# A fused retention layer on one core: masked scores over 512 tokens, against two chunks joined by a state, with the keys transposed by VectorE and moved by DMA

## What is computed

```python
qkv = silu(xn @ qkv_w.T)                       # q, k, v per head, 128 wide
scores = (q @ k.T) * decay                     # decay: exp(-slope_h * (n - m)) for n >= m, else 0
attn = scores @ v                              # the reference does it in blocks of 32 with a state
attn = norm_w * attn * rsqrt(mean(attn**2) + 1e-5)
x = x + (sigmoid(xn @ gate_w.T) * attn) @ out_w.T + ffn(xn)
```

## Time and profile before

| | |
|---|---|
| runs | 1080.37, 1080.43, 1080.39 us; median 1080.39 |
| profiled execution, span from the first to the last instruction | 1078.5 us (a time of its own is not listed beside it) |
| PE busy | 1072.7 us, 99% |
| weight loads of PE (beside it) | 946.2 us, 88% |
| DVE, ACT, POOL busy | 681.0, 702.6, 633.4 us (63%, 65%, 59%) |
| DMA | 60.05 MB, mean 56 GB/s |
| granted clock of PE | 1.000 |

### The profile page before, as it was taken

How to read it: one execution, slowest core, us unless ns; L and a number is a source line. 1 busy time by engine, 2 the same in 40 slices (tenths; PEclk the granted TensorE clock), 3 DMA queues, 4 the chain that set the end, 5 groups by cost and what they waited for, 6 DMA issues and landing times.

```text
span 1078.5 us, 19035 instructions
## 1 busy us (share of the span) xinstructions
PE 1072.7 (99%) x5938; PEld 946.2 (88%) x5938; DVE 681.0 (63%) x1150; ACT 702.6 (65%) x1463; POOL 633.4 (59%) x625
## 2 busy tenths in 40 slices
PE   8999999999999999999999999999999999999999
PEld 7998889888898888988898888988889888898898
DVE  6876664657556575665755666465755657566566
ACT  9677665766657665675756766576666756567642
POOL 5548563684737647375544846367473764647655
PEclk9999999999999999999999999999999999999999
DMA  8112020120202111021201102011020211102122
GB/s 304 65 45 84 25 64 21 45 64 26 64 19 70 57 34 54 7 80 39 61 26 44 63 24 63 19 44 63 24 69 14 82 44 44 45 30 77 55 90 79
DMA packets 41606, 60.05 MB, mean 56 GB/s; under 512 B 3936, under 2 KB 21600, under 8 KB 41568
## 3 DMA queue, kind: packets, MB, share of 16 engines
q1 hardware_dynamic: 41280, 59.05, 16.9%
q10 hardware_dynamic: 288, 0.52, 0.1%
HBM read 52.74 MB, written 6.82 MB: 55 GB/s over the span
## 4 chain that ended last, share of the span: by engine, by line
PE 98%; DVE 1%; ACT 0%; POOL 0%; DMA 0%; issue 0%; DVEq 0%; POOLq 0%
PE bank_q L1834 8%; PE bank_q L1836 8%; PE bank_q L1835 8%; PE bank_p L1834 6%; PE bank_p L1836 6%; PE bank_r L1834 6%; PE bank_p L1835 6%; PE bank_r L1836 6%; PE bank_r L1835 6%; PE outp L1834 5%; PE outp L1835 5%; PE outp L1836 5%; PE score L1836 3%; PE score L1835 3%; PE score L1834 3%; PE att L1836 3%
## 5 line engine op out<-in xcount | busy, mean ns | idle before, releaser
L419 POOL TENSOR_TENSOR w_lo<-combo,w_hi 128x768 fp32r<-128x768 f32 (+1 forms) x128 | 166.7, 1310 | 147.6 <-ACT w_hi L615 147.4
L419 POOL TENSOR_TENSOR w_lo<-raw,w_hi 128x256 fp32r<-128x256 f32 (+1 forms) x128 | 131.5, 1029 | 131.1 <-ACT w_hi L615 130.6
L1398 DVE TENSOR_TENSOR acc<-acc,outp 128x512 f32<-128x512 f32 x116 | 79.4, 685 | 74.7 <-PE outp L1836 73.7
L470 POOL TENSOR_TENSOR sum_sq<-sum_sq,square 128x512 f32<-128x512 f32 x64 | 82.8, 1293 | 66.6 <-ACT square L771 66.6
L1835 PE MATMUL bank_q<-c_lo,w_hi 128*128 128x512 f32 x276 | 107.4, 389 | 0.0
L1836 PE MATMUL bank_q<-c_hi,w_lo 128*128 128x512 f32 x276 | 107.4, 389 | 0.0
L1834 PE MATMUL bank_q<-c_hi,w_hi 128*128 128x512 f32 x276 | 107.4, 389 | 0.0
L615 ACT ACTIVATE p_hi<-score 128x896 fp32r<-128x896 f32 (+1 forms) x128 | 81.1, 649 | 33.9 <-DVE score L1306 33.0
L1306 DVE TENSOR_TENSOR score<-score,table 128x512 f32<-128x512 f32 (+1 forms) x128 | 75.9, 627 | 41.7 <-PE score L1836 40.7
L1257 DVE TENSOR_TENSOR xs<-bank_r,xs 128x512 f32<-128x512 f32 x64 | 44.2, 690 | 88.6 <-ACT xs L615 60.9
L1834 PE MATMUL outp<-wo_hi,g_hi 128*128 128x512 f32 x250 | 97.6, 390 | 0.0
(11 more groups left out here) (304 smaller groups left out, 3460.8 us busy)
## 6 DMA issues: line engine op xcount, KB each, us to landing
raw<-w_chunks SPq DMA_DIRECT2D x165, 256.0 KB, 2.9
near_dram<-near SPq DMA_DIRECT2D x2, 2048.0 KB, 9.8
table<-near_dram SPq DMA_DIRECT2D x32, 128.0 KB, 2.0
y<-x SPq DMA_DIRECT2D x8, 256.0 KB, 3.2
out<-acc SPq DMA_DIRECT2D x7, 256.0 KB, 2.0
acc<-x SPq DMA_DIRECT2D x6, 256.0 KB, 5.4
acc<-x ACTq DMA_DIRECT2D x2, 256.0 KB, 3.8
hw_dram<-acc SPq DMA_DIRECT2D x1, 512.0 KB, 2.6
```

Of the source, the lines that this page charges most:

```text
L419: pool.tensor_tensor(piece(w_lo[i % 2], j), piece_source(i, j), piece(w_hi[i % 2], j).bitcast(F32), ALU.subtract).then_inc(wlo[j], 1)
L470: pool.tensor_tensor(sum_sq[:, s % 2, :], sum_sq[:, s % 2, :], square[:], ALU.add).then_inc(summed, 1)
L1398: dve.tensor_tensor(tile, tile, outp, ALU.add).then_inc(acc_done, 1)
```

## The change

The 512 tokens of a sequence are cut into two chunks of 256. Within a chunk, scores and attention are done as before, in blocks of 128: per chunk one even key block against 256 queries in fp32r, and one odd block of 128x128 in plain fp32. What chunk 1 gets from chunk 0 goes through a state of 128x128:

- `turn_keys(s)` (DVE) transposes chunk 0's keys in blocks of 32x32; `move_keys(g, s)` (SP) writes them to DRAM in four DMAs, waits for these, and reads them back in two, as keys_t[token, dim];
- `keys(s)` (ACT) scales keys_t by the decay to the chunk's end; `state(s)` (PE) is keys_t times the values, in plain fp32, in the bank `side`;
- `state_high(s)` (ACT), `state_low(s)` (DVE) split it; `inter(s)` (PE) multiplies it with the queries of chunk 1;
- `fade_cross(s)` (DVE) scales that by the decay since the chunk's start (`fade`, one row per head, `load_fade` on SP), `add_cross(s)` (DVE) adds it to the second half of `att`; squares wait for att_whole.

Both chunks use one table of 256 columns, so the masks are two instructions over both, `probs` and `probs_lo` one each, and `make_far` goes. keys_t, state_hi, state_lo, cross and side exist once. All scalars and narrow tiles are moved, so that each operand of a matmul starts at a multiple of 512 bytes. The core of the diff:

```diff
+            def load_fade(head):
+                at_least(sp, cross_made, 2 * head)
+                sp.dma_start(fade[:], near_dram[bass.ds(head, 1), 0:1].rearrange("a p n -> (a p) n").to_broadcast([P, HALF])).then_inc(fade_in, 16)
+
+            def move_keys(g, s):
+                sp.wait_ge(k_turned, STEPS * g + s + 1)
+                for i in range(D // 32):
+                    sp.dma_start(keys_dram[s % 2, :, i, :].rearrange("(j t) n -> t j n", j=4),
+                                 k_blocks[32 * i:32 * i + 32, :].rearrange("t (j n) -> t j n", j=4)).then_inc(keys_out, 16)
+                sp.wait_ge(keys_out, 64 * (STEPS * g + s + 1))
+                at_least(sp, state_made, STEPS * g + s)
+                for a in range(2):
+                    sp.dma_start(keys_t[:, a, :].rearrange("p (i c) -> p i c", c=32), keys_dram[s % 2, :, :, 32 * a:32 * a + 32]).then_inc(keys_in, 16)
...
             def body(g, first=False, final=False):
+                move_keys(g, 0)
                 unit_taken(g, V1)
                 load_rows(0, 20 * g + 5, 20 * g + 6)
                 unit_taken(g, V2)
                 load_rows(1, 20 * g + 10, 20 * g + 12)
+                move_keys(g, 1)
                 load_near(4 * g + 1)
                 unit_taken(g, QK1)
                 load_rows(0, 20 * g + 8, 20 * g + 9)
+                load_fade(4 * g + 1)
                 unit_taken(g, QK2)
                 load_rows(1, 20 * g + 13, 20 * g + 17)
+                move_keys(g, 2)
+                move_keys(g, 3)
...
+                def keys(s):
+                    N, h = STEPS * g + s, s // 2
+                    act.wait_ge(keys_in, 32 * (N + 1))
+                    act.wait_ge(fades_now, g + 1)
+                    copy(keys_t[:, 0, :], keys_t[:, 0, :], scale=k_fade_now[:, 0, h:h + 1])
+                    copy(keys_t[:, 1, :], keys_t[:, 1, :], scale=k_fade_now[:, 1, h:h + 1]).then_inc(k_faded, 1)
...
+                def turn_keys(s):
...
+                    at_least(dve, keys_out, 64 * N)
+                    dve.transpose(k_blocks[:, :].rearrange("p (j a c) -> p j a c", a=2, c=32),
+                                  k_all[b][:, 0:HALF].rearrange("p (a j c) -> p j a c", a=2, c=32)).then_inc(k_turned, 1)
...
+                    at_least(pe, plo_done, N)
+                    for a in range(2):
+                        pe.matmul(score[:, a, HALF:HALF + P], k_all[b][:, a * HALF + P:a * HALF + HALF], q_odd[b][:, a, :],
+                                  start=True, stop=False, skip_group_check=True)
+                    if with_state:
+                        state(s)
+                    for a in range(2):
+                        mm = three(score[:, a, 0:HALF], k_hi[b][:, a, :], k_lo[b][:, a, :], q_hi[b][:, a * HALF:a * HALF + HALF],
+                                   q_lo[b][:, a * HALF:a * HALF + HALF], False, True)
+                    mm.then_inc(scored, 1)
...
+                def state(s):
+                    N, b, r = STEPS * g + s, s % 2, s // 4
+                    pe.wait_ge(k_faded, N + 1)
+                    at_least(pe, cross_made, N)
...
+                    for t in range(2):
+                        mm = pe.matmul(side[:, HALF:HALF + D], keys_t[:, t, :], v_01[r, b][:, t, head_cols(s)], start=t == 0, stop=t == 1,
+                                       skip_group_check=True)
+                    mm.then_inc(state_made, 1)
+
+                def inter(s):
+                    N, b = STEPS * g + s, s % 2
+                    pe.wait_ge(slo_done, N + 1)
+                    three(side[:, 0:HALF], state_hi[:], state_lo[:], q_hi[b][:, HALF:], q_lo[b][:, HALF:], True, True).then_inc(cross_ready, 1)
...
                     prod(QK2, 6)
                     output(-1)
-                    prod(QK2, 2, 5, 7)
+                    state(2)
+                    prod(QK2, 2, 5)
+                    prod(QK2, 7)
+                    inter(2)
                     attend(2)
                     prod(QK2, 4)
                     scores(3)
                     prod(QK2, 3)
                     prod(G23, 1)
+                    state(3)
```

More of the change, by code:

```diff
@@ L47 @@
 BANK_AT = {(0, 0): "p", (0, 1): "r", (1, 0): "q", (1, 1): "x"}
-P_LEN = tuple(SEQ - P * j for j in range(TB))
-P_AT = tuple(sum(P_LEN[:j]) for j in range(TB))
-P_COLS = P_AT[TB - 1]
-S_ORDER = (0, 1, 3, 2)
-A_ORDER = (0, 1, 3, 2)
-K_COLS = (TB - 1) * P
+HALF = 2 * P
 G_AT = (0, 1, 2, 0, 2, 1, 0, 2)
@@ L130, in build @@
         square = sb("square", [P, SEQ])
-        table = sb("table", [P, SEQ])
-        ident = sb("ident", [P, P])
-        ones = sb("ones", [P, 1])
-        slope = sb("slope", [P, HEADS])
-        far = sb("far", [P, 2, HEADS])
-        norm = sb("norm", [P, HEADS])
-        half_norm = sb("half_norm", [P, HEADS])
-        norm_now = sb("norm_now", [P, 4])
-        far_now = sb("far_now", [P, 2, 4])
-        minus_half = sb("minus_half", [P, 5 * NTB])
-        rs = sb("rs", [P, 4, NTB])
-        q_hi, q_lo, k_hi, k_lo, q_last, k_last, y = ([None] * BATCH for _ in range(7))
+        table = sb("table", [P, HALF])
+        fade = sb("fade", [P, HALF])
+        k_blocks = sb("k_blocks", [P, HALF])
+        keys_t = sb("keys_t", [P, 2, D])
+        state_hi = sb("state_hi", [P, D], F32R)
+        state_lo = sb("state_lo", [P, D], F32R)
+        cross = sb("cross", [P, HALF])
+        q_hi, q_lo, k_hi, k_lo, q_odd, k_all, y = ([None] * BATCH for _ in range(7))
         for b in range(BATCH):
@@ L1988, in body @@
                     output(-3)
-                    prod(V2, 2, 7, 5, 4, 3)
+                    state(0)
+                    prod(V2, 2, 7)
+                    prod(V2, 5, 4, 3)
+                    inter(0)
                     attend(0)
@@ L1992, in body @@
                     output(-2)
-                    scores(1)
-                    prod(QK1, 2, 7, 5, 4, 3)
+                    scores(1, with_state=True)
+                    prod(QK1, 2, 7)
+                    prod(QK1, 5, 4)
+                    prod(QK1, 3)
+                    inter(1)
                     attend(1)
@@ L2029, in body @@
                     output(7)
-                    prod(QK0, 2, 5, 7)
+                    prod(QK0, 2)
+                    state(6)
+                    prod(QK0, 5, 7)
+                    inter(6)
                     attend(6)
@@ L2034, in body @@
                     prod(QK0, 3)
+                    state(7)
                     output(8)
+                    inter(7)
                     prod(G01, 1, 6)
@@ L2076, in body @@
                 prod(G23, 1)
+                state(3)
                 output(0)
-                prod(G23, 6, 2)
+                prod(G23, 6)
+                prod(G23, 2)
                 output(1)
+                inter(3)
                 attend(3)
@@ L2106, in body @@
                 output(8)
-                prod(G01, 1, 6)
+                state(7)
+                prod(G01, 1)
+                inter(7)
+                prod(G01, 6)
                 output(9)
```

653 lines of the change are left out of this document (351 added, 302 removed).

## The result

| | before | after |
|---|---|---|
| median of the runs | 1080.4 us (4 runs) | 1158.0 us (4 runs, 1153.0 to 1158.6) |
| ratio, 95% interval | | 1.071 [1.069, 1.073] |
| span of the profiled execution | 1078.5 us | 1156.4 us |
| PE busy / without work in the span | 1072.7 / 5.8 us | 1083.6 / 72.8 us |
| mean granted clock of PE | 1.000 | 0.973 |

What follows compares the result with a forecast made beforehand. TensorE, busy 1072.7 of 1078.5 us, was taken as the bound, with no slack for waits. 1080.4 - 29 (matmuls) + 8 x (4.2 + 2.0 + 0.5) (waits) = 1105 us, range 1082 to 1138.

Steps and rivals of the forecast that it cites:

- Matmuls, -29 forecast: TensorE's cheaper scores and attention, less state and its product, win 0.45 us a step, 29 us over 64 steps.
- The four parts: Matmuls per step after the change: scores 1.16 us, attention 1.16, state 0.44, its product with the queries 0.36; sum 3.12.
- a product stays at 1.36: On TensorE, each product was taken to keep its 1.36 us, and an output tile like it.
- The wait at state(2): TensorE waits 4.2 us a group at step 2's state for keys coming through DRAM and ScalarE's fade.
- The short trip of 5.5 us: Lower bound of a keys' trip through DRAM, taken as 6.2 us within 5.5 to 8.0, from 1.8 us per landing.
- Step 3: Late keys 3 hold ScalarE, so q's low part is late for G23's first product: TensorE waits another 2.0 us a group.
- Output 8: Waits for step 6's g_lo: 0.5 us a group, between 0 and 1.1, after 0.9 us of slack.
- For six of the eight steps the trip starts early enough: Keys' trips through DRAM: only steps 2 and 3 were followed as short; the other six were taken to be in time.
- Start and tail "do the same work": Start and tail were given no cost, but for one added pass before the last outputs, hidden by them.
- rival 3: Each 4.2 us pause brings a slow TensorE clock, costing 1.7 us, 8 x 1.7 = 14: 1119 us; chance 0.14.
- Two operands in SBUF: Low parts of k and first v chunk read two SBUF operands: up to 0.4 us on the chain, left to range.
- Rivals 1, 2 and 4: Rival 1: keys in time, 1052 us, chance 0.11; 2: short trips, 1083, 0.15; 4: slow small packets, 1147, 0.10.

Runs made afterwards that it cites:

- run 2: Changed kernel without the keys' turn, DRAM trip and fade, the state made from a constant tile: 1082.7 us, ratio 1.003.
- the last version: Changed kernel with every operation kept and only orders changed, after the last of several sets of moves: 1074.2 us, ratio 0.994 against the kernel before.
- run 4: Changed kernel with idle matmuls ahead of state(2): 60 took 1166.6 us, 36 took 1152.5; with keys 3 turned early, 1159.3 without idle matmuls, 1144.9 with 36.
- run 5: Changed kernel, keys 2 earlier in SP's queue: 1142.2 us; second, also keys 2's fade ahead of a weight copy on ScalarE: 1143.5 us.
- run 6: Changed kernel, last group's order only: fade row behind the router's weights, last output weights' low part ahead of two bias additions: 1147.2 us.
- run 7: Changed kernel, all operations kept, only orders changed, in successive sets of moves: 1100.3, 1079.8, 1078.2, then 1074.2 us.
- run 1: Changed kernel, state made from a constant tile without TensorE's wait for the keys, ScalarE still waiting for them: 1164.1 us.
- run 3: Changed kernel, keys' turn and DRAM trips kept, but no fade, no engine waiting for keys, state from a constant tile: 1092.3 us.

## Why the forecast was wrong in size

The side was right, and so was the mechanism that it put first. Three things failed: the half clock and the waits at state(5) and at the end, which the sum had at nothing, and the price of a product. By its own steps, with the 1105 of the sum against 1158:

- **Matmuls, -29 forecast.** 14 given back. The four parts were right: in run 2 scores and attention start to start are 1.17 us each, the state 0.36 and its product 0.37, some 3.1 a step where I had 3.12. What failed is "a product stays at 1.36". In the last version's timeline of PE:

```profile
465.07 0.71 PE L1991 MATMUL side<-v,keys_t 128*128 128x128 f32 x4
465.54 0.48 PE L1910 MATMUL bank_p<-b_hi,w_hi 128*128 128x512 f32 x1
465.86 0.40 PE L1911 MATMUL bank_p<-b_lo,w_hi 128*128 128x512 f32 x1
...
467.00 0.39 PE L1910 MATMUL bank_r<-c_hi,w_hi 128*128 128x512 f32 x1
```

  A product behind a state takes 1.46 us, its first matmul 0.32 for 0.23: the switch back from plain fp32, which I had priced inside scores and attention only. Behind scores it takes 1.39 (462.02 to 463.41), where before it took 1.36 there too (327.47 to 328.83). Six of eight states stand ahead of a product or an output, so the switch makes 48 x 0.10 + 128 x 0.03, some 9 us, less the 64 x 0.04 just named. The matmuls are worth 2.6 us a group without trips and 2.0 with them (125.1 and 125.7 against 127.7), and over the whole span 14 with them, 15 short. What the switch leaves of the 15 is open; a part can be short waits that count as busy, since the ends of matmuls are modelled.
- **The wait at state(2), 8 x 4.2 = 34.** Measured 4.7 each, 37.9 in all. Right, with its causes. There was some luck in it: the way out landed in 1.6 us for the 2.0 assumed, the way in 2.4, and the two errors cancel. (The short trip of 5.5 us does not come out of its own terms: with 1.8 us a landing the sum is 5.8.)
- **Step 3, 8 x 2.0 = 16.** Measured 0.8 in all. Not wrong as a chain (10.2 us in run 4, 23.7 in the second of run 5), but covered by the slow stretch in front of it.
- **Output 8, 8 x 0.5 = 4.** 8.2, in seven waits; with the cause that was forecast, and twice its size.
- **State(5).** "For six of the eight steps the trip starts early enough" failed here: 8 x 1.14 = 9.1 us. I had looked for the short trips; these keys had landed long before, and their fade stood behind squares(4) on ScalarE. Of a moved step I followed what it waits for, and not its place in the queue of the engine that does it.
- **Start and tail "do the same work".** It failed: 5.2 + 2.7 + 1.4 + 0.8 = 10 us of waits, of which run 6 takes away the first two, and 10.8 us with the slow stretches at them. y's new reader, and a queued load in front of the router's weights, were both in the diff.
- **The clock, rival 3.** The sum had it at nothing; I gave it 0.14 and 1.7 us a pause. 25 us of busy time are lost to it. The size came from the one slow stretch that the trace before had, 4.4 us at the start; at the pauses the clock is half for 3.4 or 6.8 us, 2.9 to 6.1 of them with PE busy (2.3 us lost at each of the eleven), and eleven pauses have it, not eight. Its net price is less, 5.5 us in place. The Trainium skill (TensorE: Matmul & The Clock Gate, HAM oscillation) says that idle gaps between bursts bring the clock down; the trace agrees, with 0.50 behind every one of the eight pauses, and the rival should have had a higher chance.
- **Two operands in SBUF.** Left to the range. The low part of k takes 575 ns for 256 columns, where 384 columns from a bank took 552, so that part of the cost came; what it adds on the chain was not tested.

The parts: idle 67 for 54, matmuls -14 for -29, clock 25 for 0; 13 + 15 + 25 = 53 = 1158 - 1105. Rivals 1, 2 and 4 fell: no keys in time, trips not short enough, landings at 1.6 and 2.4, not 2.9. The claim that there is no slack to pay a wait from held. That the waits come with the operations did not: run 7 has all of the operations and hardly a wait.

## What to carry over

On an engine that is busy all the time, list for every added step its place in each in-order queue (the engine's, and SP's) and ask what stands in front of it and behind it, not only when its data arrive; and look at every tile that shares its address with one whose last reader moves. A wait on such an engine may be covered by the one before it: removing one shows the next, so price the whole chain, and expect to need several moves before the time follows. Here the same operations took 1158 us in one order and 1074 in another.

## What was not expected of the hardware

- At each pause of 4.4 us or more in the changed kernel PE's granted clock fell to 0.50, 2.0 to 4.7 us after PE's last matmul, and stayed there for 3.4 or 6.8 us; it did so at one of 2.1 and one of 2.7 us too. Over the traces of all these runs, of 182 pauses of 0.9 to 1.8 us (1.77 the longest) none had such a stretch in it or up to 2 us behind it, and all of the 48 of 3.1 us or more (3.12 the shortest) had one. In between it went either way, 26 of 41: 1.79 us in run 1 with, 3.11 us in run 3 without. With idle matmuls in the gap it stayed at 1.00 in seven of the eight groups.
- With a part of the operand tiles off multiples of 256 bytes the kernel was 0.4 to 0.8% slower; matmuls that read none of the moved tiles were longer too (393 ns for 389). Which access meets which was not tried.
- A fp32r matmul of 128 columns in a stream took 0.11 us (60 in 6.8 us, the first of run 4), one of 256 takes 0.12.
- The way out in packets of 256 bytes landed in 1.6 us and the way in with packets of 128 bytes in 2.4, around the 2.0 of the 128 KB table. VectorE's block transpose of 128x256 takes 0.435 us, near the 0.426 of a mask over as many columns.
